# Two 128x512 products of constants per tile in the first attention of a transformer kernel

## The reference

```python
Q = (x_text @ Wq).reshape(Bb, Tt, 4, 32)
K = (x_vision @ Wk).reshape(Bb, Gg, 4, 32)
scores = einsum('bthd,bghd->bhtg', Q, K) / sqrt(32)
scores = where(vision_mask, scores, -inf)
topv, topi = top_k(scores, 32)
probs = softmax(topv)                       # of the 32 largest of 64
attn = zeros_like(scores).at[..., topi].set(probs)
c_t = (attn.mean(heads) @ (x_vision @ Wv)) * text_mask
x = layernorm(x_text) * (1 + mod_gate * scale_in) + mod_gate * shift_in    # from c_t @ W_film_in
y = s4d(x, ...)                             # a convolution along the tokens, one kernel per channel
y = y * (1 + mod_gate * scale_out) + mod_gate * shift_out                  # from c_t @ W_film_out
```

## Time and profile before

| | |
|---|---|
| Median of 3 runs | 938.84 us (936.86 to 939.61) |
| Span of the profiled execution | 935.4 us |
| PE busy | 710.3 us, 6072 matmul records |
| DVE busy | 673.2 us |
| First attention, PE's first to last instruction | 23.7 to 257.4 us |
| Convolution, PE | 259.73 to 287.25 us |

### The profile page before, as it was taken

The page is one execution under the profiler, slowest core; times in us unless marked ns, Lnnn a source line. Parts: engine busy times, 40 slices in busy tenths (PEclk is TensorE's granted clock), DMA queues, the critical chain, the costliest instruction groups (busy, mean ns, idle before and its releaser), DMA issues. The chain is left out here.

```text
span 935.4 us, 20537 instructions
## 1 busy us (share of the span) xinstructions
PE 710.3 (76%) x6072; PEld 508.4 (54%) x6072; DVE 673.2 (72%) x3212; ACT 473.4 (51%) x1318; POOL 564.8 (60%) x931
## 2 busy tenths in 40 slices
PE   0686898979883999972498528998888874799970
PEld 0353554545483656631275426766666652699970
DVE  6898989978524688769111167598998887699974
ACT  3566576735200455450133175577777761577740
POOL 7688877766526544210677667345777767277770
PEclk9767787957555999996599855798988885899995
DMA  6300112997213977700365330000000002698928
GB/s 143 57 25 10 41 45 64 86 88 96 40 45 140 290 250 257 243 23 0 39 115 132 88 137 1 2 4 13 25 26 25 25 28 76 216 279 264 260 69 270
DMA packets 98829, 94.41 MB, mean 101 GB/s; under 512 B 37511, under 2 KB 82302, under 8 KB 98142
## 3 DMA queue, kind: packets, MB, share of 16 engines
q1 hardware_dynamic: 91268, 79.34, 33.1%
q0 software_dynamic: 6592, 13.58, 6.0%
q10 hardware_dynamic: 858, 0.17, 0.1%
HBM read 47.76 MB, written 43.19 MB: 97 GB/s over the span
## 5 line engine op out<-in xcount | busy, mean ns | idle before, releaser
L2402 POOL DMA_INDIRECT expert_pairs<-e_ys,e_home x78 | 75.4, 967 | 38.4 <-issue 23.5
L1742 POOL TENSOR_SCALAR a_kb<-a_kr,a_m,a_bk 128x128 f32<-128x128 f32 x128 | 57.9, 452 | 44.4 <-ACT a_kr L1981 32.3
L1760 POOL DMA_INDIRECT expert_slots<-r_rows,r_slotu x64 | 63.3, 989 | 30.3 <-DVE r_rows L2136 15.1
L950 DVE MATCH_REPLACE8 work<-m,work 128x64 f32<-128x64 f32 x384 | 75.7, 207 | 0.0
L1484 POOL DMA_INDIRECT ex_rows<-rows,slot_source x32 | 30.7, 960 | 52.7 <-POOLq L1163 43.2
L937 DVE MAX8 m<-work 128x8 f32<-128x64 f32 x384 | 57.0, 209 | 0.0
L825 PE MATMUL psf<-filmw,us 97*128 97x512 f32 x64 | 51.6, 902 | 3.0 <-ACT FO L846 2.9
L1815 PE MATMUL a_pss<-a_kb,a_qt 32*64 32x256 f32 x512 | 41.5, 463 | 13.9 <-ACT a_pp L1966 11.7
L2168 DVE TENSOR_REDUCE a_mx<-a_pss 128x8 f32<-128x512 f32 x64 | 43.9, 686 | 8.1 <-PE a_pss L1815 7.8
L2369 PE MATMUL e_ps<-e_XH,e_wh 128*128 128x256 f32 x156 | 48.1, 308 | 1.5 <-DVE e_XL L2414 1.5
L1536 ACT ACTIVATE ex_hs<-ex_psh,vec 128x512 f32<-128x512 f32 x32 | 22.0, 687 | 51.2 <-PE ex_psh L1517 50.5
(11 more groups left out here) (464 smaller groups left out, 2418.2 us busy)
## 6 DMA issues: line engine op xcount, KB each, us to landing
expert_slots<-rt_unfilled SPq DMA_DIRECT2D x151, 130.0 KB, 2.6
ahead<-folded_weights SPq DMA_DIRECT2D x20, 386.0 KB
e_wf<-folded_weights SPq DMA_DIRECT2D x19, 386.0 KB, 4.2
planes<-rt_zeros SPq DMA_DIRECT2D x4, 1024.0 KB
ew<-in_L_ffn_ew SPq DMA_DIRECT2D x16, 256.0 KB, 4.0
pair_y<-expert_pairs SPq DMA_DIRECT2D x16, 256.0 KB, 5.6
e_xr<-expert_slots SPq DMA_DIRECT2D x27, 130.0 KB, 3.3
folded_weights<-fold_done SPq DMA_DIRECT2D x8, 384.0 KB, 4.3
```

What stands on the lines that cost most here:

```text
L950: return own.did(dve.match_replace(wk_[x.j][:, h, :], m8[x.j][:, h, r, :], src[:, h, :], TAKEN))
L1742: m = pool.tensor_scalar(kb[a.j][:, :, h, :], k, m4[:, h:h + 1], bk4[:, h:h + 1], ALU.mult, ALU.add)
L1760: pool.indirect_dma_start(G.slots, bass.IndirectOffsetOnAxis(ap=slot[:, b, k, t:t + 1], axis=0), rb[b % NB][:, k, t, :], None).then_inc(se ...
L2402: pool.indirect_dma_start(G.pair, bass.IndirectOffsetOnAxis(ap=home[i % NY][:, k:k + 1], axis=0), ys[i % NY][:, k, :], None).then_inc(kept ...
```

## The change

Ahead of each side piece of tile 0 and later, PE now multiplies the constant ones (as weights) with the first 512 columns of the penalties into the bank `side`, twice; ahead of a "second" piece once, ahead of a "first" piece not at all. The piece that follows overwrites the bank, so the products are read by no one. In the four slots without a piece there are two products as well, behind a wait for ACT to have kept the last piece (34), and three more stand at the end of PE's stage. That is 38 + 8 + 3 = 49 products of 128x512. No other engine's instructions change.

```diff
--- before.py
+++ after.py
@@ -630,6 +630,10 @@
                 return ("turn", "first", "second")[(n - 13) % 3], 1 + (n - 13) // 3
             return None, 0
 
+        NSIDE = 13 + 3 * (NE - 1)
+        FILL = {"first": 0, "second": 1}
+        held = G.pen[:, 0:512 // T, :].rearrange("p n t -> p (n t)")
+
         def made(name, part=0):
 
             return 1 + [side_job(n) for n in range(13 + 3 * (NE - 1))].index((name, part))
@@ -768,11 +772,20 @@
 
             @block.tensor
             def _(pe):
-                def side_piece(n):
+                def warm(t, n):
+
+                    for _ in range(n if t >= 0 else 0):
+                        pe.matmul(side[:], G.ones[:], held, start=True, stop=True)
+
+                def side_piece(t):
+                    n = t + 3
                     name, e = side_job(n)
                     if name is None:
+                        after(pe, s["side_kept"], NSIDE)
+                        warm(t, 2)
                         return
                     after(pe, s["side_kept"], n)
+                    warm(t, FILL.get(name, 2))
                     if name == "mask":
                         mm = pe.transpose(side[:, 0:NT], K.tmf, G.ident[0:NT, 0:NT])
                     if name == "values":
@@ -832,13 +845,14 @@
                         pe.wait_ge(s["turned_sb"], qk.t + 1)
                         pe.matmul(psa[j][:, 256:384], G.wq[:], xf[j][:], start=True, stop=True)
                         pe.matmul(psa[j][:, 384:512], G.wk[:], cf[j][:], start=True, stop=True).then_inc(s["qk"], 1)
-                    side_piece(x.t + 3)
+                    side_piece(x.t)
                     if attn.real():
                         pe.wait_ge(s["attn"], attn.t + 1)
                         after(pe, s["u_sb"], attn.t - 1)
                         pe.transpose(psb[attn.j][:, 0:P], at[attn.j][:], G.ident[:]).then_inc(s["attn_turned"], 1)
 
                 march(slot, -3, NT + 3)
+                warm(0, 3)
 
             @block.scalar
             def _(act):
```

## The result

The changed kernel takes 930.02 us (median of 14 runs, 916.85 to 940.26) against 938.64 us in the same rounds; the ratio is 0.988, 95% interval 0.984 to 0.992. Medians here are of all runs, while the ratios leave out runs more than 1.5% above the fastest of their kernel, to which the profiled executions of the changed kernel, `tail_only`, `first_zero` and `end_two` belong. The medians differ by 8.6 us (the ratio alone would give 11); forecast were 930.5 and a sum of -8.5. The sum is right, its terms are not: in the profiled executions the attention gave less and the convolution more.

The account below looks back on a forecast made before the run. It took DVE to set the first attention's pace, with PE holding it up when its clock fell. Terms of -6.5 (attention), +1.5 (stage end) and -3.5 (convolution) gave -8.5 us, 930.5; 8-in-10 range 921 to 945.

Parts of the forecast that it names:

- DVE sets the pace, PE steps in when its clock falls: Attention stage: DVE's slot of one tile, 6.07 us, sets the pace; PE holds it up when its clock falls.
- In the cycles, "turn" and "second" have room for the products: Side work's three-slot cycle: with the products PE is busy 18.0 us against DVE's 18.2, covered with no room.
- -9 us of waits, +2.5 of new ones (-6.5): Attention up to DVE's last slot: 9 us of DVE waits go, 1.5 and 1 us come, -6.5 us.
- the 15.2 us: Attention stage: DVE waits of 21.0 us, less pipeline filling and a DMA wait; the most that could go.
- +1.5 for the end of the stage: Behind the side work: convolution starts 0.9 to 2.8 us later against DVE's end, taken as +1.5.
- the case "low" of the working: End of the stage, clock low: tile 30's transpose starts +2.7 us later; upper end for the convolution's start, 2.8.
- -3.5 for the convolution: Convolution starts at the high level and keeps it about 3.3 us, each us saving one; bounds 0 and 13.7.
- The rival of -13.7 us: Convolution keeps the high level to its end, saving 13.7 us; 920 us in all, chance 0.12.
- PE the bound: Attention cycles: the products make PE slower than DVE, +9 us, 948 us; chance 0.13.
- zeros: The added products multiply zeros and so do not hold the clock; same price of +9 us, chance 0.06.
- wash: Stalls in attention and stage end only change places: -2 to +2 us, 938 us; chance 0.22.
- The signs: Expected in the profile: DVE waits 8 to 15 us, convolution some 5 us earlier, 3 to 5 us at full clock.

Follow-up runs that it names:

- tail_only: The changed kernel without the 38 products ahead of side pieces, keeping the eleven behind the side work; 931.07 us, ratio 0.991.
- first_zero: The changed kernel with six products at the end instead of eleven, plus one ahead of expert 0's first piece (tile 4); 922.54 us, ratio 0.985.
- end_two: The changed kernel with only two products behind the pieces, at the end, instead of eleven; 926.58 us, ratio 0.988.
- thin: The changed kernel with weights of 32x32 and 32 rows in the same 49 products of 512 columns; 999.17 us, ratio 1.050.
- data: The changed kernel with columns of the input x (random numbers) in place of zeros as moving operand; 923.49 us, ratio 0.987.
- again: The changed kernel, unaltered, run once more beside three other kernels; 928.45 us, ratio 0.990.
- tail_six: The changed kernel with no products ahead of side pieces and six at the end (two each at tiles 32 and 33, two last); 926.85 us, ratio 0.989.
- slots_only: The changed kernel with only the 38 products ahead of side pieces, without the eleven behind the side work; 934.10 us, ratio 0.995.
- turn_only: The changed kernel with six products at the end instead of eleven, and none ahead of the second pieces; 922.21 us, ratio 0.985.

## Why the prediction was right, and where its terms were not

- *DVE sets the pace, PE steps in when its clock falls*: held. With as many columns to multiply and the clock down (`thin`) the kernel lost 5.0%, 47 us.
- *In the cycles, "turn" and "second" have room for the products*: held; 4.90 and 4.74 us of work in "turn", no "first" that starts low in the cycles shown.
- *-9 us of waits, +2.5 of new ones (-6.5)*: too large. The waits fell by 3.7 us, DVE's last slot came 2.5 us earlier here, and the slots alone brought 4.1 us on the median (934.10 against 938.17). Two parts of the 15.2 us that I held for removable stayed: those ahead of tiles 5 to 7 (5.2 us after 4.3), and those from 180 us on (9.4 after 10.5), among them the waits where the products stand behind the DMA that makes PE idle. For the first part no reason is shown: with the same products it is 1.6 us in `data`. The spread of single executions of the same 38 products (242.8 to 246.8 us in the table, 250.8 in `end_two`) is as large as the term, and so is that of DVE's waits: 14.3 to 23.7 us with slot products, 17.8 to 26.7 without.
- *+1.5 for the end of the stage (0.9 to 2.8 for the convolution's start)*: too small. Against DVE's last slot it was 3.8 us here, 3.8 in `again` and 3.7 in `tail_only`: the case "low" of the working (2.8) and one more us, since the film product behind the first pair still ran low: from 248.79 to 255.45 the two slots took 6.7 us, not 5.8. With the level high at tile 30 (`data`) it was 1.3.
- *-3.5 for the convolution*: too small; -5.5 here, -6.9 to -9.2 in `tail_only`, `again` and `data`, and up to -12.4 in `tail_six`. What failed was the nearest row: the thin products of "first" lost the level behind 3.3 us, the convolution's passes kept it for 9 to 14 us, and in two executions to the end. The factor was 1.8 rather than two (29.5 to 31 against 53 ns). L829 was read as bound by its weights, but its 0.43 us for 128 columns is a quarter of L825's 1.71 for 512, so that row goes with the columns. And PE's gaps took up to 1.5 us back. The rival of -13.7 us, with a chance of 0.12, had the better mechanism, though only two of eleven profiled executions went that way.
- *PE the bound, zeros, wash*: for this change refuted by the interval of the result, the zeros by `data` too. `thin` shows that the price of the first is real, and far larger than worked out.
- *The signs*: the convolution did not start 5 us earlier but 1.3 us later (261.07 against 259.73), 10 us of it and not 3 to 5 were at 1.00, and DVE's waits (17.3 us, 19.2 in `again`) lie between the 8 to 15 expected and the 21 that would have shown the prediction wrong.
- *The 62 ns of the sequencer*: as a bound on a pass no run here shows it, since the passes ran at 29.5 to 31 ns. The Trainium skill (TensorE: Matmul & The Clock Gate, section "Wait — 56ns, not 53.3ns?") gives about 62 ns a matmul with hardware decoding off. Whether it was off is not on record, and a product of two passes took 59 to 62 ns, so the rule is not refuted if it counts products.
- *A reading*: of the slices said to mix the two levels the ninth has 5, the low one alone.

So the terms were off by +4, +2.3 and -2 to -6 us. In the two profiled executions of the changed kernel they sum to -4.2 and -5.3 us; that the medians differ by the forecast -8.5 is in part luck.

## What to carry to other kernels

A product of constants is worth its time where it stands just ahead of dense work that would else start at the low level: six products here bought, within the noise, what 49 did. Put it where PE waits for nothing that comes later, never behind the wait that makes PE idle and never ahead of the instruction for which the next engine waits. Products that keep PE busy with a small part of the array are worse than none.

## What the runs showed of the hardware

- The clock does not follow PE's busy time: 43.92 us busy of 44.00 with weights of 32x32 among the rest had 0.54, while cycles with idle time and products on the whole array had 1.00.
- Zeros as operand hold the level as random numbers do, within the intervals (ratios 0.988 and 0.990 against 0.987, and 0.984 against 0.987 with six products at the end).
- Passes of 64x64 weights over 32 columns never raised the level in 27.5 us (before, `slots_only`, `thin`), and kept it for up to 15.7 us once it was up (`turn_only`; 15.1 in `tail_six`, to the last pass). Where the level fell, it fell behind a gap of PE of 0.49 us or more, in nine executions of nine.
- These gaps ("issue", 0.27 to 1.48 us, after 97 to 391 passes) stand only at the high level, and PE went on 1.2 to 1.5 us after a 16 KB block of instructions had landed, in 12 gaps of 12.
